# Four edits to the last stage of a graph network kernel: where stores are issued, which units are split, and the order of the last two tiles of a search

## The reference

```python
z = leaky_relu(lap_mul(A, h) @ W1 + b1)      # lap_mul(A, x) = d * (A @ (d * x)), d = 1 / sqrt(row sums of A)
d2 = sq[:, None] + sq[None, :] - 2.0 * (z @ z.T)
S = exp(-sqrt(max(d2, 0) + 1e-10) / 2)
S = where(ranks < 4, S, 0)                    # the four largest of each row
out = lap_mul(S + A, h) @ W2 + b2
```

## Time and profile before

| | us |
|---|---|
| median of 3 runs without a profile | 1427.34 (1426.28 to 1427.92) |
| the profiled execution, its own time | 1422.04 |
| its span, first to last instruction | 1420.1 |
| TensorE busy in the span | 1324.5 (93%) |
| VectorE busy | 1118.1 (79%) |
| ScalarE busy | 745.1 (52%) |
| GpSimd busy | 154.3 (11%) |
| mean granted TensorE clock | 0.979 of full speed |

### The profile page before, as it was taken

The page is one execution under the profiler, slowest core; times in us unless marked ns, Lnnn a source line. Parts: engine busy times, 40 slices in busy tenths (PEclk is TensorE's granted clock), DMA queues, the critical chain, the costliest instruction groups (busy, mean ns, idle before and its releaser), DMA issues.

```text
span 1420.1 us, 15414 instructions
## 1 busy us (share of the span) xinstructions
PE 1324.5 (93%) x5434; PEld 960.0 (68%) x5434; DVE 1118.1 (79%) x1528; ACT 745.1 (52%) x1118; POOL 154.3 (11%) x146
## 2 busy tenths in 40 slices
PE   7999999999899999999999999989999999828995
PEld 4556677788678767777787778766777775415663
DVE  7987888898999888766557988599999996306555
ACT  2322232446666668666547777456665652405554
POOL 0000000000000000000000000000000000567884
PEclk9999999999999999999999999999999999968998
DMA  9777666558767776665558899201111116639993
GB/s 340 238 257 242 225 209 195 189 182 293 252 237 236 268 263 196 207 209 192 185 177 281 271 327 341 91 0 39 51 52 52 52 52 200 232 110 349 387 385 143
DMA packets 82860, 291.49 MB, mean 205 GB/s; under 512 B 10848, under 2 KB 10976, under 8 KB 82784
## 3 DMA queue, kind: packets, MB, share of 16 engines
q1 hardware_dynamic: 78048, 280.01, 57.5%
q0 software_dynamic: 4736, 10.49, 2.4%
HBM read 286.27 MB, written 4.19 MB: 205 GB/s over the span
## 4 chain that ended last, share of the span: by engine, by line
PE 61%; DVE 28%; issue 4%; another core or an unknown queue 3%; ACT 3%; DMA 1%; POOL 1%; SPq 0%; ACTq 0%; POOLq 0%
PE ps L451 14%; PE ps L446 13%; PE ps L448 13%; PE ps L447 12%; DVE best_at L1163 9%; DVE rows_T L1161 9%; DVE A_lo L1086 5%; PE ps L521 1%; PE ps L549 1%; PE ps L550 1%; PE ps L484 1%; PE ps L490 1%; DVE hn L942 1%; PE ps L508 1%
## 5 line engine op out<-in xcount | busy, mean ns | idle before, releaser
L1086 DVE TENSOR_TENSOR A_lo<-ring,A_hi 128x1024 fp32r<-128x1024 f32 x369 | 439.4, 1218 | 109.1 <-ACT A_hi L661 91.4
L661 ACT ACTIVATE A_hi<-ring 128x1024 fp32r<-128x1024 f32 x369 | 381.1, 1056 | 165.0 <-PE ps L448 96.9
L446 PE MATMUL ps<-A_hi,G_odd_hi 128*128 128x512 f32 x602 | 258.3, 429 | 34.2 <-DVE A_lo L1086 31.2
L448 PE MATMUL ps<-A_hi,G_odd_lo 128*128 128x512 f32 x602 | 236.9, 394 | 1.0 <-issue 1.0
L447 PE MATMUL ps<-A_lo,G_odd_hi 128*128 128x512 f32 x602 | 235.7, 392 | 0.2 <-issue 0.2
L661 ACT ACTIVATE scores<-ps,neg_sq 128x1024 f32<-128x1024 f32 x128 | 137.6, 1112 | 52.9 <-PE ps L622 37.2
L446 PEld LDWEIGHTS ps<-A_hi,G_odd_hi 128*128 128x128 f32 x602 | 113.9, 189 | 70.7 <-issue 50.2
L451 PE MATMUL ps<-ring,G_last 128*128 128x512 f32 x332 | 155.9, 601 | 5.2 <-ACT G_last L661 3.7
L446 PE MATMUL ps<-A_hi,G_even_hi 128*128 128x512 f32 x368 | 153.6, 417 | 0.2 <-DVE A_lo L1086 0.2
L1273 POOL DMA_INDIRECT landing<-scaled_rows,best_at x128 | 143.8, 1124 | 46.9 <-issue 38.4
L1161 DVE MAX8 rows_T<-scores 128x8 f32<-128x4096 f32 x32 | 141.3, 4415 | 7.0 <-ACT scores L661 7.0
(11 more groups left out here) (134 smaller groups left out, 1411.9 us busy)
## 6 DMA issues: line engine op xcount, KB each, us to landing
ring<-adj_t SPq DMA_DIRECT2D x524, 512.0 KB
X<-x_rows SPq DMA_DIRECT2D x8, 256.0 KB, 7.0
scaled_rows<-G_last POOLq DMA_DIRECT2D x8, 256.0 KB, 2.7
landing<-scaled_rows,best_at POOLq DMA_INDIRECT x128
out_rows<-X SPq DMA_DIRECT2D x8, 256.0 KB
pack<-packed SPq DMA_DIRECT2D x1, 836.0 KB, 15.3
pack<-packed SPq DMA_DIRECT2D x1, 192.0 KB, 4.1
```

The lines of the kernel that those rows point to most:

```text
L446: mm(acc, G_hi[odd][:, kb, t, :], hi, start=start, stop=False)
L448: done = mm(acc, G_lo[odd][:, kb, t, :], hi, start=False, stop=stop)
L661: return nc.scalar.activation(out_ap, in_ap, func, **k)
L1086: v_.tensor_tensor(A_lo[:, s, :, :], ring[:, s, :, :], A_hi[:, slot_of(v), :, :].bitcast(fp32), ALU.subtract).then_inc(lower_ready, 1)
```

## The change

The stores leave the load loop: all eight stand behind the last load. In the stage after the search a unit is split where `u` is 4 or 12, 11 of 94 in place of 45. `early` is gone: no unit is prepared ahead of `similarity` and `new_degrees` of the last block. VectorE takes the values of the last two tiles first, then clamps, and finds their places with `last_rest` and `new_degrees` between. The constants of `near_due` change: tile t is due at unit (8.0 + 5.2 t) / 1.7 in place of (10 + 5.8 t) / 1.6, and the last tile of a block no sooner than unit 13 and 8 units behind the last unit of its block.

```diff
--- before.py
+++ after.py
@@ -58,7 +58,10 @@
 
 
 
-LAST_US, NEAR_US, NEAR_FIRST = 1.6, 5.8, 10.0
+LAST_US, NEAR_US, NEAR_FIRST = 1.7, 5.2, 8.0
+
+
+SPLIT_EVERY = 8
 
 
 class Plan:
@@ -106,13 +109,15 @@
         for b in range(2, NB):
             for u in range(UNITS):
                 if b > 2 or u not in ended[:6]:
-                    self.last_visit(b, u, u % 2 == 0)
+                    self.last_visit(b, u, u % SPLIT_EVERY == SPLIT_EVERY // 2)
         opened = sorted(self.spans, key=lambda g: (self.spans[g][0], g[0]))
         self.bank = {g: i % BANKS for i, g in enumerate(opened)}
         self.bank_before = {g: opened[i - BANKS] for i, g in enumerate(opened) if i >= BANKS}
         self.near_due = {}
         for t in range(NT):
             at = self.search_end + int((NEAR_FIRST + NEAR_US * t) / LAST_US)
+            if t % TPB == TPB - 1:
+                at = max(at, self.search_end + 13, self.spans[4, t // TPB, 4][1] + 8)
             self.near_due.setdefault(min(at, len(self.visits)), []).append(t)
         self.split_count, n = {}, 0
         for v in self.visits:
@@ -346,8 +351,6 @@
         free = [k for k in range(2 * BANKS) if k not in (PLAN.bank[4, 0, 4], PLAN.bank[4, 1, 4])]
         score_banks = (free[0:2], (AUX, AUX + 1), (TB, GB))
 
-
-        early = next(v for v in PLAN.visits[PLAN.search_end:] if v.split)
         first_hn = (hn, nat)
         first_hT, first_G = (TB, AUX), (GB, AUX + 1)
 
@@ -371,7 +374,6 @@
                 sp.wait_ge(x_final, b + 1)
                 sp.dma_start(out[b, :, :, :], X[:, b, :, :]).then_inc(out_stored, 16)
 
-            sent = 0
             load_x(0)
             sp.dma_start(pack[:, 0:3 * P], pack_in[:, 0:3 * P]).then_inc(pack_loaded, 16)
             load_x(1)
@@ -383,11 +385,7 @@
             sp.dma_start(pack[:, 3 * P:PACK], pack_in[:, 3 * P:PACK]).then_inc(rest_loaded, 16)
             for v in PLAN.visits[SLOTS:]:
                 load_unit(v)
-                for t in PLAN.near_due.get(v.n - SLOTS - 2, ()):
-                    if t % TPB == TPB - 1:
-                        send(t // TPB)
-                        sent += 1
-            for b in range(sent, NB):
+            for b in range(NB):
                 send(b)
             sp.wait_ge(out_stored, 16 * NB)
 
@@ -898,13 +896,11 @@
             pair_out(TPB * m + 2)
             pair_out(TPB * m + 3)
             scale_last(m - 1)
-            act.wait_ge(scanned, NT - 1)
-            upper(early)
             similarity(m)
             new_roots(m)
             scale_last(m)
             for v in PLAN.visits[PLAN.search_end:]:
-                if v.split and v is not early:
+                if v.split:
                     upper(v)
                 if v.n - PLAN.search_end in (6, 10):
                     move_out(4, (v.n - PLAN.search_end) // 4 - 1)
@@ -1153,14 +1149,17 @@
                 for name, p, b in PLAN.due["DVE"][n]:
                     step(name, p, b)
 
+            def scan_values(i):
+                dve.wait_ge(evicted, 4 * i + 4)
+                own.add(v_.max(best[:, seek[i], :], scores[i % 2][:, :]))
+
+            def scan_places(i):
+                own.settle()
+                v_.max_index(best_at[:, seek[i], :], best[:, seek[i], :], scores[i % 2][:, :]).then_inc(scanned, 1)
+
             def scan(i):
-
-                t = seek[i]
-                dve.wait_ge(evicted, 4 * i + 4)
-                row = scores[i % 2][:, :]
-                own.add(v_.max(best[:, t, :], row))
-                own.settle()
-                v_.max_index(best_at[:, t, :], best[:, t, :], row).then_inc(scanned, 1)
+                scan_values(i)
+                scan_places(i)
 
             def clamp(m):
                 b = seek_blocks[m]
@@ -1221,17 +1220,19 @@
                     new_inverse(i // TPB - 1)
                 elif i >= TPB:
                     last_rest(i // TPB - 1)
+
             m = NB - 1
-            scan(NT - 2)
+            scan_values(NT - 2)
+            scan_values(NT - 1)
+            clamp(m)
+            scan_places(NT - 2)
             last_rest(m - 1)
-            scan(NT - 1)
-            clamp(m)
-            lower(early)
             new_degrees(m)
+            scan_places(NT - 1)
             new_inverse(m)
             last_rest(m)
             for v in PLAN.visits[PLAN.search_end:]:
-                if v.split and v is not early:
+                if v.split:
                     lower(v)
                 for t in PLAN.near_due.get(v.n, ()):
                     weigh(t)
```

## The result

| | us |
|---|---|
| changed kernel, median of 4 | 1447.54 (1447.02 to 1449.5) |
| kernel before, median of 4 beside it | 1427.63 |
| ratio, 95% interval | 1.0135 (1.0106 to 1.0163) |

The changed kernel is 1.35% slower. Forecast were 1388 us and a range of 1381 to 1419; the measured time lies outside, on the other side of the kernel before. It is the time of the third rival, 1448 us, which had a chance of 0.07. Each timed execution comes with its own span and clock, so those that are called "without a profile" above were recorded too, and the 5.3 us between the profiled execution of before and the median were the spread of executions.

What follows compares the result with a forecast made beforehand. TensorE and GpSimd's gathers both bind, ending near 1405. TensorE's 1404.9 minus 5.6, 29.1, 1.3 and 9.5 plus 11.6 gave 1371.0; the tail made 1380.3, plus 1.9 and 5.3 gave 1387.5, forecast as 1388, range 1381 to 1419.

Steps and rivals of the forecast that it cites:

- third rival: TensorE during the gathers: the hole comes back repeatedly, some 30 us each; two give 1448 us; chance 0.07.
- The sum: Whole span: TensorE's last unit near 1371, then the tail, without the hole: 1380.3 us; chance 0.53.
- The hole: TensorE idle for 29.11 us until 1283.24, plus 1.3 of low clock; no instruction found that explains it; summed without it.
- The hole comes back once: One such TensorE stop after the search, priced 29.1 + 1.3 us: 1410.7 in the span, 1418 us; chance 0.27.
- second rival: GpSimd's gathers stay at 1.47 us, slowed by ring traffic and not subtractions: 1402.8 in the span, 1410 us; chance 0.10.

Runs made afterwards that it cites:

- e17: Changed kernel with one unit in two split after the search, on a stalling chip: 1416.7 us, ratio 0.9928.
- spaced kernel: Changed kernel with a waited-for memset on GpSimd after each gather, so gathers come 1.50 us apart: 1409.4, 1408.9 and, on a stalling chip, 1408.7 us.
- e7: Changed kernel with each unit after the search loaded by four DMAs of 32 partitions in place of one of 128, on a stalling chip: 1473.7 us, ratio 1.033.
- e8: Changed kernel with the stores between the loads again, on a stalling chip: 1447.6 us, ratio 1.0142.
- e13: Changed kernel with each gather replaced by a plain DMA of 128 fixed rows from the same GpSimd queue, on a steady chip: 1382.4 us.
- e10: Changed kernel with one unit in four split after the search, on a stalling chip: 1440.3 us, ratio 1.0077.
- e18: Changed kernel with gathers for the first eight of 32 tiles only, on a stalling chip: 1398.6 us, one execution.

## Why the prediction was wrong

**What came true, on the chips without slow stretches.** The sum was 1380.3 us in the span; it was 1383.0, and the median time 1383.8 us, inside the range. The 5.3 us that took the sum from 1382.2 to 1388 were not there: the profiled execution (1384.9) lies beside its median. By step: the inverse was forecast at 1199.0 and came at 1198.7. The first gather was forecast at 1203.6 and came at 1206.4, because GpSimd waited 5.2 us for the store of the scaled rows and not the 2.2 us of the earlier trace rows: DMA traffic was at 324 GB/s in this wait of the changed kernel, and at 86 in that of the kernel before, where TensorE had stood for `G_last`. The gathers were forecast at 165.6 us and took 168.0. TensorE's last unit was forecast for 1371.0 and ended at 1373.4, with 1.6 us of waiting for a subtraction and 0.7 for a transpose that were not in the sum. The tail behind it took 9.6 us, 9.3 in the sum. As parts, against the kernel before on steady chips: the new order of the last tiles 9.6 us, the due places and stores with one unit in two split perhaps 3 more (0.9910 against 0.9929, intervals that overlap), and one in eight some 11 more (0.9835 against 0.9910). The last was counted as a loss on TensorE of 11.6 us that freed the gathers. It also took away TensorE's waits for subtractions, 16.3 us with 45 of them and 1.6 with 11.

**The step that failed** is *The hole*: "The change names nothing that made it [...] I sum without it". It was the main thing: the same changed kernel takes 1383.8 us without slow stretches and 1447.5 with them, so the term that was put at nothing measured 64 us. The trace of before showed a stalling chip, and its hole was made by GpSimd's first 44 gathers, issued at 1.28 us. It was cleared when the eight slots were full. Later in that trace the subtractions held 84 gathers at 1.50 us, and nothing happened. The change takes 34 of 45 subtractions away, and with them the brake. With them back, the changed kernel goes on a stalling chip from 1.0135 of the kernel before to 0.9928 (e17). The prediction counted this as a gain (gathers 17 us shorter) and, in the third rival, described its price rightly: place, rate, the stop at a full slot, 30 us a hole, 1448 us. Its total fits better than its parts: it had two holes of 30 us. By TensorE's transposes (L482) the changed kernel lies 40 us behind its steady trace after the first stretch (1283.9 against 1243.4), 57 after the second (1355.1 against 1297.9) and 63 after the last (1389.8 against 1327.0), so there were three stops of 40, 17 and 6 us; that their sum came to 1448 is in part luck. The prediction gave this rival 0.07 against 0.53 for the sum. Two facts at hand spoke for a higher chance: the hole was in the only trace there was, and the median of the kernel before (1427) lay 14 us above what its own sum without a hole gave (1413; steady chips gave 1406).

That the runs of before "probably have it too" was right: on steady chips the kernel before takes 1406 us, on stalling ones 1425 to 1429. *The hole comes back once* and *repeatedly* were split wrongly: after each stop the changed kernel's gathers start again at 1.25 to 1.3 us, and nothing in the change speaks for a single hole.

**The second rival**, gathers at 1.47 us by ring traffic, fell: with 11 subtractions they took 1.31 us beside 338 GB/s. The rule of the Trainium skill that was weighed for the gathers (SBUF — State Buffer, Who interferes with whom) holds in direction; the mean price of a subtraction was 0.5 us in the kernel before and 0.75 us here (129.2 - 128 x 0.945 = 8.2 us over 11), and not a whole instruction of 1.22 us.

**What is not settled.** The mechanism in the chip is not shown. That increments leave no record while the gathers run, and only on the chips on which TensorE is slowed, suggests one path that both use, the recording itself among the suspects; all times here are of recorded executions, and no run tells what an unrecorded one does. The spaced kernel on a stalling chip also loses records and is not slowed, so the loss alone does not make the slow stretch. More increments did not bring it sooner (e7), within what that confounded run can say. Plain DMAs of GpSimd ran only on a steady chip (e13), so whether it takes the indirect form is open. Each chip ran in one batch only, so a lasting property of the chip is argued and not shown.

**Which kernel is best.** On a steady chip the changed one (1384 us). On a stalling one only e7 is slower and e8 equals it, and the spaced one beats both: 1408.7 us against 1425 and 1447. The spaced kernel takes 1408.7 to 1409.4 us on all three chips that it ran on; the price is 25 us on steady ones.

## What to carry to other kernels

An engine that slows another one down can be a brake that something needs: before removing work from it, ask at which rate the freed engine will run, and look in the trace for what happened when it already ran at that rate. A stall in the trace that no dependency explains is the first thing to price, not to leave out of the sum; a median that lies above the sum without it is evidence that it is in every run. And measure on more than one chip, and again at another time, when a gain of 1 to 2% hangs on it: here the sign turned from one batch to the next.

## What the runs showed of the hardware that was not expected

On two of the five chips of this study, and in the first measurement, a series of indirect DMAs from GpSimd, each 1.25 us after the last, slows TensorE after 21 or 22 of them (25.5 to 27.3 us in e8, e10, e18 and the changed kernel): an instruction begins only every 0.7 to 2.1 us, whether it is a matmul, a transpose or a load of weights. The granted clock falls to its lower level, 1.2 GHz, 3 to 5 us later and stays there until TensorE is quick again. The slow stretch ended 3.5 us after the last gather in the eight-tile kernel (1245.8 and 1249.3), and some 10 us after a first series of 48 in e8 and e10 (1267.2 and 1278, 1266.3 and 1276). At 1.50 us it does not happen in 128 of them. On the other three chips it does not happen at 1.31 us either, over 168 us.

While the gathers run on such a chip, semaphore increments of DMAs are missing from the record, from the first gather on and so before TensorE slows. The same kernel differs by 0.1% or less between steady chips (1394.7 and 1394.6 us, 1409.4 and 1408.9), and between a steady and a stalling one by nothing if its gathers are spaced to 1.50 us, by 1.5% for the kernel before and by 4.6% for the changed one.
